# The up pass loads h as two stored fp16 parts, and 40 of 48 gate units are finished beside it

## The reference

```python
x = act_qdq(x)                                   # h: 16 bit integers times one scale
up = act_qdq(x @ lpbq_dequant(w_up).T)           # 1536 columns
gate = act_qdq(x @ lpbq_dequant(w_gate).T)
sig = fixed_qdq_u16(jax.nn.sigmoid(gate))
gate = act_qdq(gate * sig)
o = act_qdq(gate * up)
return o @ lpbq_dequant(w_down).T
```

## Time and profile before

| | us |
|---|---|
| median of 3 runs | 2348.25 (2347.79 to 2348.65) |
| span of the profiled execution | 2347.3 |
| the median less that span | 0.95 |
| opening (attention) up to the first gate matmul | 646.9 |
| gate stage | 646.9 to 1146.1 |
| up pass | 1146.3 to 1643.7 |
| no matmul | 1643.7 to 1836.8 |
| down pass to the end | 1836.8 to 2347.3 |

### The profile page before, as it was taken

One profiled execution on the slowest core, in us unless ns is written; L12 is line 12 of the kernel. 1 busy time (PEld: TensorE's weight loads), 2 busy tenths in 40 slices (PEclk: granted clock), 3 DMA queues, 4 the chain that ended last, 5 costly groups with the idle time before them and its releaser, 6 DMA issues.

```text
span 2347.3 us, 25386 instructions
## 1 busy us (share of the span) xinstructions
PE 2020.4 (86%) x9524; PEld 945.0 (40%) x9524; DVE 1715.7 (73%) x1387; ACT 1398.2 (60%) x1599; POOL 670.6 (29%) x662
## 2 busy tenths in 40 slices
PE   5888888888599999999999999999000699999998
PEld 2444444444244444444444444444000344444443
DVE  8799999999634534532499998999899644577641
ACT  4678887887422322322499996676899633366530
POOL 2599999998300000000121110222111000000000
PEclk9999999999799999999999999999555899999999
DMA  7789999998346656743699995787998755555541
GB/s 297 283 314 337 348 337 346 335 350 316 126 181 226 225 207 223 259 148 144 242 378 390 378 369 209 264 320 293 401 419 327 291 229 208 205 201 232 233 152 72
DMA packets 131162, 634.60 MB, mean 270 GB/s; under 512 B 12256, under 2 KB 12768, under 8 KB 91104
## 3 DMA queue, kind: packets, MB, share of 16 engines
q1 hardware_dynamic: 85888, 316.81, 37.0%
q0 software_dynamic: 45152, 316.16, 34.6%
HBM read 430.69 MB, written 202.24 MB: 270 GB/s over the span
## 4 chain that ended last, share of the span: by engine, by line
PE 64%; issue 3%; DVE 3%; ACT 2%; POOL 0%; DVEq 0%; ACTq 0%; POOLq 0%
PE fd_pp L1777 42%; PE fd_pp L1791 21%; ACT ff_ring L1720 1%; DVE ff_sig L1575 1%; DVE ff_h_parts L1559 1%; DVE ff_sq L1497 1%; ACT ff_sig L1707 0%; DVE ff_sq L1566 0%; DVE kept_gate L1568 0%; DVE ff_gin L1510 0%; DVE ff_hq L1549 0%; ACT ff_hq L1632 0%; ACT ff_ring L1746 0%; ACT ff_sig L1736 0%; DVE kept_o_peak L1575 0%
## 5 line engine op out<-in xcount | busy, mean ns | idle before, releaser
L1791 PE MATMUL fd_pp<-ff_down,kept_gate 128*128 128x512 f16 x1536 | 458.9, 381 | 193.1 <-DVE ff_up L1616 193.1
L1777 PE MATMUL fd_pp<-ff_h_parts,kept_gate 128*128 128x512 f16 x2304 | 499.6, 380 | 14.3 <-DVE ff_h_parts L1415 14.3
L1777 PE MATMUL fd_pp<-ff_h_parts,ff_up 128*128 128x512 f16 x2304 | 497.4, 379 | 0.0
L1639 ACT ACTIVATE ff_raw<-fd_pp 128x1024 f32<-128x1024 f32 x192 | 194.3, 1017 | 396.5 <-PE fd_pp L1777 396.5
L1777 PEld LDWEIGHTS fd_pp<-ff_h_parts,kept_gate 128*128 128x128 f16 x2304 | 225.9, 98 | 287.9 <-DVE ff_h_parts L1415 14.7
L1777 PEld LDWEIGHTS fd_pp<-ff_h_parts,ff_up 128*128 128x128 f16 x2304 | 225.4, 98 | 271.8
L1420 DVE TENSOR_REDUCE kept_gate_peak<-ff_raw 128x1 f32<-128x2048 f32 x48 | 109.7, 2285 | 292.9 <-ACT ff_raw L1639 292.9
L1791 PEld LDWEIGHTS fd_pp<-ff_down,kept_gate 128*128 128x128 f16 x1536 | 150.6, 98 | 375.9 <-issue 195.8
L1791 PE MATMUL fd_pp<-ff_down,ff_up 128*128 128x512 f16 x768 | 292.2, 380 | 0.0
L1746 ACT ACTIVATE ff_ring<-ff_hq,kept_g 128x2048 int16<-128x2048 f32 x48 | 96.0, 1999 | 191.1 <-DVE ff_hq L1549 189.7
L790 PE MATMUL at_psO<-kept_wo,at_ahi 128*128 128x512 f16 x512 | 155.5, 386 | 36.2 <-ACT at_alo L277 31.6
(11 more groups left out here) (239 smaller groups left out, 3454.9 us busy)
## 6 DMA issues: line engine op xcount, KB each, us to landing
ff_raw<-up_scratch SPq DMA_DIRECT2D x66, 1024.0 KB, 8.5
gate_scratch<-ff_raw POOLq DMA_DIRECT2D x48, 1024.0 KB, 9.1
ff_gin<-gate_scratch SPq DMA_DIRECT2D x48, 1024.0 KB, 8.7
up_scratch<-ff_raw POOLq DMA_DIRECT2D x48, 1024.0 KB, 7.7
ff_gin<-gate_integers SPq DMA_DIRECT2D x73, 512.0 KB, 5.8
gate_integers<-ff_ring POOLq DMA_DIRECT2D x43, 512.0 KB, 8.7
ff_up<-up_scratch SPq DMA_DIRECT2D x21, 1024.0 KB, 9.5
kept_xs<-in_x SPq DMA_DIRECT2D x32, 512.0 KB, 14.6
```

Of the source, the lines that this page charges most:

```text
L1639: nc.scalar.activation(raw[:, n % UNITS, h * 2 * BLK:(h + 1) * 2 * BLK], pp[(2 * n + h) % 4][:, :, :].rearrange("p a t -> p (a t)"), ACT.C ...
L1777: mm = nc.tensor.matmul(pp[k % 4][:, h, :], wt[w][:, c, f:f + P], a[:, b % 2, :, c, :], start=(q == 0), stop=(q == len(todo) - 1))
L1791: mm = nc.tensor.matmul(pp[k % 8 // 2][:, k % 2, :], a[b % 2][:, f, t * P:(t + 1) * P], wt[w][:, f, :], start=(q == 0 and i == 0), stop=(q ...
```

## The change

- READY goes from 36 to 40, so 40 of the 48 units are finished in the up pass, SECOND falls from 30 to 28, and the planner lays out order, made and the slots anew.
- split runs in the gate stage alone. POOL stores its two parts (store_parts, 1024 KB a block) in place of the int16 (512 KB), after split's second instruction.
- In the up pass SP loads the two parts straight into h_parts (load_parts), and PE waits for that load in place of DVE. The load of a block waits until PE has finished the block that used the buffer.
- On SP the loads of h stand behind the gate loads of the same step; before, they stood ahead of them.
- split(b) waits for the store of the parts of block b-2; quantise doesn't wait for a store any more.

```diff
--- before.py
+++ after.py
@@ -35,7 +35,7 @@
 UN = 4
 UNITS = FC // UN
 UE = UN * BLK
-READY = 36
+READY = 40
 EARLY = 4
 XR = 9
 KEPT = 8
@@ -923,7 +923,7 @@
     return mem
 
 
-def feed(nc, keep, mem, hT_d, hq_d, gate_d, up_d, gate_q, x1_d, out, NB, scale_d, mats):
+def feed(nc, keep, mem, hT_d, parts_d, gate_d, up_d, gate_q, x1_d, out, NB, scale_d, mats):
 
 
 
@@ -1044,8 +1044,8 @@
         fo_oq = ring[:, 2, :]
         xb = flat(t_h[:, :, :, :, :, :]).bitcast(F32).rearrange("p (b n d) -> p b n d", b=2, n=SUB)
 
-        h_in, hq_out = [s.sem(f"h_in{i}") for i in range(2)], [s.sem(f"hq_out{i}") for i in range(2)]
-        hq_in = [s.sem(f"hq_in{i}") for i in range(2)]
+        h_in, parts_out = [s.sem(f"h_in{i}") for i in range(2)], [s.sem(f"parts_out{i}") for i in range(2)]
+        parts_in = [s.sem(f"parts_in{i}") for i in range(2)]
         stored = [s.sem(f"stored{i}") for i in range(UNITS)]
         nat_in, piece_in = [s.sem(f"nat_in{i}") for i in range(2)], [s.sem(f"piece_in{i}") for i in range(2)]
         gate_in, gq_out = [s.sem(f"gate_in{i}") for i in range(GR)], [s.sem(f"gq_out{i}") for i in range(QR)]
@@ -1100,6 +1100,10 @@
             r = (v - KEPT) % AR
             return wide[:, r, :] if r < 2 * GR else ring[:, 0, :]
 
+        def parts(b):
+
+            return t_h[:, :, b % 2].rearrange("p a n c t -> p a (n c t)")
+
         def stored_first(r):
 
             return len(range(r, AWAY, QR))
@@ -1203,13 +1207,13 @@
                             sp.dma_start(dst[32 * a:32 * a + 32, k % 2, :].rearrange("p (c o) -> p c o", o=o),
                                          by_quarter[a, j * rows:(j + 1) * rows, :].partition_broadcast(32)).then_inc(piece_in[k % 2], 16)
 
-                def load_hq(b):
+                def load_parts(b):
 
                     if b < NB:
-                        sp.wait_ge(m["al"], NB + b - 1)
+                        sp.wait_ge(m["mm"], (NB + b - 1) * PAIRS)
                         if b < 2:
-                            sp.wait_ge(hq_out[b], 16 * (NB // 2))
-                        sp.dma_start(hq[:, b % 2, :], hq_d[b]).then_inc(hq_in[b % 2], 16)
+                            sp.wait_ge(parts_out[b], 16 * (NB // 2))
+                        sp.dma_start(parts(b), parts_d[b]).then_inc(parts_in[b % 2], 16)
 
                 def load_gate(u):
                     if u < NU:
@@ -1296,14 +1300,14 @@
                     if q == 0:
                         sp.wait_ge(m["peak"], n + 1)
                         load_h(b + 2)
-                load_hq(0)
                 for u in range(GR):
                     load_gate(u)
+                load_parts(0)
                 for n in range(NU):
-                    if n % UNITS == 0:
-                        load_hq(n // UNITS + 1)
                     for u in first_units(n):
                         load_gate(u + GR)
+                    if n % UNITS == 0:
+                        load_parts(n // UNITS + 1)
                     if n >= SECOND:
                         sp.wait_ge(m["peak"], NU + n - 1)
                         load_again(2 * (n - SECOND))
@@ -1324,9 +1328,9 @@
 
             @block.gpsimd
             def _(pool):
-                def store_h(b):
-                    pool.wait_ge(m["hq"], b + 1)
-                    pool.dma_start(hq_d[b], hq[:, b % 2, :]).then_inc(hq_out[b % 2], 16)
+                def store_parts(b):
+                    pool.wait_ge(m["al"], b + 1)
+                    pool.dma_start(parts_d[b], parts(b)).then_inc(parts_out[b % 2], 16)
 
                 def store_raw(n):
                     pool.wait_ge(m["peak"], n + 1)
@@ -1350,19 +1354,19 @@
                     u = order[i]
                     need(pool, m["prod"], max(prior + 1, i - NEAR))
                     if kind == "wq" and prior < 0:
-                        pool.wait_ge(m["al"], 2 * NB)
+                        pool.wait_ge(m["al"], NB)
                         pool.wait_ge(m["gpeak"], NU)
                     if not late(u):
                         pool.wait_ge(again_out[u % AR], 16 * (u // AR + 1))
                     pool.dma_start(gated(i), gate_q[u]).then_inc(g_in[kind, j], 16)
 
                 soon = [i for i in loaded[:WQ] if late(order[i])]
-                store_h(0)
+                store_parts(0)
                 for n in range(NU):
                     b, q = n // UNITS, n % UNITS
                     store_raw(n)
                     if q == 0 and b + 1 < NB:
-                        store_h(b + 1)
+                        store_parts(b + 1)
                     i, k = lane(n)
                     if k == 1:
                         pool.wait_ge(m["w_red"], i + 1)
@@ -1404,11 +1408,9 @@
                 link = chain(dve, m["dve"])
 
                 def split(b):
-                    if b < NB:
-                        dve.wait_ge(m["hq"], b + 1)
-                    else:
-                        dve.wait_ge(hq_in[b % 2], 16 * ((b - NB) // 2 + 1))
+                    dve.wait_ge(m["hq"], b + 1)
                     need(dve, m["mm"], (b - 1) * PAIRS)
+                    need(dve, parts_out[b % 2], 16 * (b // 2))
                     hi, lo = (t[:, b % 2].rearrange("p n c t -> p (n c t)") for t in (ah, al))
                     nc.vector.tensor_copy(hi, hq[:, b % 2, :]).then_inc(m["ah"], 1)
                     dve.wait_ge(m["ah"], b + 1)
@@ -1457,8 +1459,6 @@
                     b, q = n // UNITS, n % UNITS
                     if q == 0 and b + 1 < NB:
                         split(b + 1)
-                    if n == NU - 2:
-                        split(NB)
                     raw_peak(n)
                     i, k = lane(n)
                     if i is not None:
@@ -1512,8 +1512,6 @@
 
                 gate_integers(1)
                 for n in range(NU):
-                    if n % UNITS == 1 and n // UNITS + 1 < NB:
-                        split(NB + n // UNITS + 1)
                     for u in first_units(n):
                         first(u)
                     if n == SECOND - 1:
@@ -1628,7 +1626,6 @@
                 def quantise(b):
                     need(act, h_in[b % 2], 16 * (b // 2))
                     need(act, m["al"], b - 1)
-                    need(act, hq_out[b % 2], 16 * (b // 2))
                     nc.scalar.activation(hq[:, b % 2, :], keep["h_first"][b] if b < 2 else hb[b % 2], ACT.Copy,
                                          scale=g[:, 1:2]).then_inc(m["hq"], 1)
 
@@ -1763,7 +1760,10 @@
             @block.tensor
             def _(pe):
                 for b in range(2 * NB):
-                    pe.wait_ge(m["al"], b + 1)
+                    if b < NB:
+                        pe.wait_ge(m["al"], b + 1)
+                    else:
+                        pe.wait_ge(parts_in[b % 2], 16 * ((b - NB) // 2 + 1))
                     wt = keep["gate" if b < NB else "up"]
                     if b == NB:
                         pe.wait_ge(m["w_lo"], PIECES)
@@ -1805,7 +1805,7 @@
 
 
     gate_q = nc.dram_tensor("gate_integers", [NB * UNITS, P + 1, UE], I16).ap()[:, 0:P, :]
-    hq_d = nc.dram_tensor("h_integers", [NB, P + 1, DC * BLK], I16).ap()[:, 0:P, :]
+    parts_d = nc.dram_tensor("h_parts", [NB, P, 2, DC * BLK], F16).ap()
     scale_d = nc.dram_tensor("weight_scales", [2, 2, F * D // QB], F32).ap()
     U3 = NB * UNITS
     with Scope(nc, "kept") as s:
@@ -1835,7 +1835,7 @@
                 for n in ("nmean", "ssq", "rstd", "shift"):
                     keep[n] = s_att.sb(n, [P, 2, 4], F32)
                 opening(nc, keep, x, ctx_t, wkv_t, idx_t, wq_t, wo_t, gate_n, tables, x1_d, hT_d, B, LKV)
-            feed(nc, keep, mem, hT_d, hq_d, gate_d, up_d, gate_q, x1_d, out, NB, scale_d,
+            feed(nc, keep, mem, hT_d, parts_d, gate_d, up_d, gate_q, x1_d, out, NB, scale_d,
                  [(up_n, up_t, "up", 5, F), (down_n, down_t, "down", 6, D)])
```

## The result

The changed kernel takes 2353.4 us, the kernel before 2348.7 in the same session (15 runs each): a ratio of 1.0021, with a 95% interval of 1.0014 to 1.0028. It is 4.7 us slower. The profiled execution has a span of 2352.4 us, where before it had 2347.3.

The account below looks back on a forecast made before the run. PE bounds all but the product pass, where DVE and ACT work is time. 4.6 + 2.5 - 11.0 + 4.5 = +0.6 us on a profiled 2347.3, 0.95 under the median, gives 2348.9 us; range 2341.5 to 2356.0.

Parts of the forecast that it names:

- rival B: Early up pass: DMA engines can't pass 386 GB/s, evictions wait for stores and PE waits, 9.5 us more, 2358.4; chance 0.13.
- What bounds the kernel: Whole kernel: PE bounds gate, up and down stages; only in the 174.5 us product pass is DVE and ACT work time.
- Part 1: Gate stage: storing 1 MB of parts per block instead of 512 KB costs 0.
- Part 2: Start of up pass: PE waits 4.6 us for block 0's parts behind gate loads, plus 2.5 us of lost clock.
- Rival A: Start of up pass: block 0's parts land before 1146.1 or nearly so; 7.1 us go, 2341.8; chance 0.11.
- Part 3: Rest of up pass: PE stays the bound, and later parts land in time; cost 0.
- Part 4: Product pass: four fewer late units shorten it by 11.0 us, bounds 9.8 and 12.0; its loads fit the bandwidth.
- a pass not shorter by ten: Product pass: sign that the prediction is wrong, meaning its loads have become its bound.
- Part 5: Seam to the down pass: first up load stands behind a wait for product 47, +4.5 us, bounds 3.5 and 5.9.
- Rival C: Seam to the down pass: costs nothing, slot waits being met earlier; 2344.4; chance 0.08.
- The down pass: Down pass: keeps its matmuls and slow start; cost 0.
- Sum: Whole kernel: 4.6 + 2.5 - 11.0 + 4.5 = +0.6 us, forecast 2348.9.

Follow-up runs that it names:

- 8: Kernel before with 40 finished units, last stage's up loads ahead of gated ones, gated loads up to ten units ahead, first ones before the pass, no parts: 2335.2 us.
- 7: Changed kernel with block 0's parts loaded first, last stage's up loads ahead of gated ones, gated loads up to ten units ahead, first ones before the pass: 2335.3 us.
- Experiment 1: Changed kernel with the load of block 0's parts issued ahead of the first four gate loads instead of behind them: 2346.5 us.
- experiment 5: Changed kernel with product-pass gated loads issued up to ten units ahead instead of seven, and the first ones before the pass: 2348.1 us.
- 6: Changed kernel with up loads of the product pass carrying only half of each unit's columns, part of the computation left out: 2349.1 us (one run).
- 9: Kernel before, 36 finished units, with gated loads up to ten units ahead and the first ones before the pass: 2348.0 us.
- 11: Changed kernel with gated loads eight units ahead instead of seven, loads issued before the pass unchanged: 2348.4 us (one run).
- 10: Changed kernel with gated loads up to ten units ahead, loads issued before the pass unchanged: 2348.8 us (ten runs).
- experiment 4: Changed kernel with the last stage's three up loads issued ahead of its three gated loads: 2349.2 us.

## Why the prediction was right and where it was not

The time lies inside the range, 4.5 us above the forecast; 0.5 us of that is the kernel before, which ran slower here (2348.7) than the prediction had it (2348.25). One step made most of the rest. That the range held it is in part luck: the product pass came out 4 us beyond its own bounds, the prediction's terms all at their worst end give 2353.5, and the range went on to 2356.0 only for the sake of rival B, which didn't occur.

*What bounds the kernel.* Right. No microsecond taken from DVE or ACT inside the up pass moved the time (with splits and without, kernels 8 and 7, it lasts 497.4 us), and those in the product pass did.

*Part 1.* Right: the gate stage took 499.7 us, before 499.6.

*Part 2.* Right in cause, and in size partly by luck: a gap of 4.9 for 4.6, and 2.5 for 2.5 of clock. The parts landed at 1151.8, 0.9 us later than foretold; but the gate stage ended at 1146.9, 0.8 us past the 1146.1 that the prediction took, which was the start of its last matmul (it ended at 1146.4). PE ran 5.1 us, from 1151.8 to 1156.9, at 0.50, inside the two stretches of the earlier trace rows. Experiment 1 shows that the place in the queue, and not the stores of raw, sets it: at the head the same 1 MB landed after 8.0 us. Rival A would have needed the parts by 1146.1; they landed 19.8 us after their issue at 1132.0.

*Part 3 and rival B.* No gap of PE in the rest of the up pass. The DMA engines moved 398 GB/s where they had moved 386, and 411 in experiment 1, all at a share of 1.00 to 1.01. So 386 was what was asked for and not a ceiling, and rival B falls.

*Part 4, the step that failed.* The term was -11.0 with bounds of -12.0 and -9.8, and the trace gave -5.9. The count of instructions was right: with the loads in time it is 11.6 (experiments 5, 6 and 9). What failed is the sentence on loads, that "spread over 163.5 us they need less than the 422 GB/s". That compares a mean with a rate. It doesn't ask how long before its use each load is issued. Call that time the lead: for a late unit, from the issue of its gated load to the moment when ACT could start its sigmoid. Here it is, over the late units whose load is issued within the pass, with the time to landing (us):

| kernel | lead | to landing | ACT waits for them |
|---|---|---|---|
| before | 9.2 to 12.2 | 3.7 to 9.9 | none, by 0.5 at the closest |
| changed | 6.7 to 10.2 | 7.9 to 9.4 | four of seven, 0.4 to 1.7 |
| half the bytes (6) | 5.1 to 10.2 | 3.6 to 5.6 | none |
| eight units ahead (11) | 12.6 to 15.8 | 8.4 to 14.1 | none, by 0.02 at the closest |

These loads didn't become slower: the four that ACT waited for landed after 8.1 to 8.4 us. The lead became shorter, and before the change it had been just enough. One late unit before (three rows) and one after (the fourth; ACT's row for it is the third of the five waits above) show how. Their loads landed after 8.0 and 8.1 us:

```profile
1683.02 0.53 POOL L1357 DMA_DIRECT2D ff_hq<-gate_integers  x1 [5.76 <-DVE kept_o_peak L1575]
1684.86 1.22 DVE L1497 TENSOR_SCALAR ff_sq<-ff_sig 128x2048 uint16<-128x2048 f32 x1
...
1692.24 1.99 ACT L1707 ACTIVATE ff_sig<-ff_hq,kept_g 128x2048 f32<-128x2048 int16 x1
```

```profile
1697.90 0.53 POOL L1361 DMA_DIRECT2D ff_hq<-gate_integers  x1 [4.71 <-DVE kept_o_peak L1573]
```

Both are issued seven units ahead. Before, DVE had still to finish the late unit four places ahead in that stretch (from 1684.86 to 1688.32, the 3.47 us of the earlier trace rows), and ACT came to the sigmoid 9.2 us after the issue. After, late units stand six places apart, that work lay ahead of the issue, and ACT was ready after 7.0 us. So seven units became a shorter time. That the lead is the cause is shown: a longer one (experiments 5, 10 and 11) or a shorter landing (6) takes these waits away. That the place of DVE's work shortened it is read from the rows and not tested by itself. The longest landing of all gated loads of the pass did grow, from 12.7 to 16.9 us, but that load was issued as the pass began, and no engine waited for it.

The prediction had named the sign, a pass not shorter by ten "which would mean its loads have become its bound", without giving it a chance or a price; and it was the time of their issue that bound, not their bytes.

The Trainium skill (DMA: Bandwidth & Descriptors, Anatomy of one DMA) gives a single transfer that GpSimd issues, as it does these loads, as about 2.0 us plus its bytes at 436 GB/s. Worked out from that page, an estimate for 512 KB is 3.2 us. The quickest load of this pass before (3.7) is near that; the median of all its gated loads after, 9.4, is three times the estimate.

*Part 5.* Right: 4.0 for 4.5, by the mechanism foretold (the first quotient follows ACT's second last_up, 9.4 us past the end of the products for 9.8); experiment 4 takes it back by moving one loop. Rival C falls.

*The down pass.* Foretold 0, measured -1.1. It is the clock: half speed from 1843.1 to 1846.4, where before it lasted from 1836.8 to 1842.4 (first row before, second after).

```profile
1836.83:1842.44 5.61, 5.61 (x14) 1.98 (x15) 3.51 (x3) 3.52 (x2) 0.00 (x0) 0.50 1.00 372
1843.09:1846.43 3.34, 3.34 (x8) 1.17 (x9) 2.05 (x1) 1.25 (x1) 0.00 (x0) 0.50 1.00 410
```

Over the 13 kernels here this stage took 498.8 to 500.2 us from its first to its last matmul, in no order that follows the edits. In each of the 13 traces that is 497.4 us plus half of the stretch at half clock at its start (2.9 to 5.6 us). Why that stretch is longer in one trace than in another is left open.

*Sum.* With 5.9 in place of 11.0 the prediction's own sum is +5.7, that is 2354.0, against 2353.4 measured.

## What to carry to other kernels

When work is taken off a stage whose DMA queues are full, compare each load's lead with the time that such a load takes to land in that stage, and not only the bytes with the bandwidth. A lead that is counted in items shrinks when the items between become cheaper, so read it from the trace, issue to use, and see how little was left before the change (here 0.5 us). A data path that is "off the critical path" still pays at the first item, where its place in the queue decides: put the load that gates the bound engine ahead of those that don't. And test a change of several parts one part at a time: here the useful part (forty units) was worth 11.6 us and was nearly hidden by two places in queues and a horizon that cost a line each.

## What was not expected of the hardware

A DMA share of 1.00 to 1.02 is not yet a bound: with the engines at that share the up pass moved 386, 398 or 411 GB/s as the kernel asked, and the product pass 417 to 421 with waits of ACT for loads (changed kernel) or with none (experiment 5). The Trainium skill (Perfetto Trace Analysis, Roofline, in its note on HBM above 100%) puts the ceiling for one core alone at about 435 GB/s; the rows agree so far as they go (422 at most), and they are above the 358 GB/s that the prediction had quoted against the change.
